# Both layer norms of a token step moved from VectorE to ScalarE, with their biases made on GpSimd

## The chip, the cores and the metric

The kernel is one program on one core of a Trainium2 chip. The time is the device time of one execution in microseconds (us). Five engines work in parallel, each through its own queue in program order: TensorE (PE, with its weight loads as PEld), VectorE (DVE), ScalarE (ACT), GpSimd (POOL) and SyncE (SP, which issues DMAs).

## The reference, cut to what matters

32 sequences of 256 steps with 64 channels pass a convolution of 9 taps (248 tokens of 128 features remain), then a Mamba-2 block and a mixture-of-experts block, both on normalised tokens and both added to the residual stream.

```python
def _layernorm(x, axis=-1, eps=1e-05):
    m = jnp.mean(x, axis=axis, keepdims=True)
    v = jnp.var(x, axis=axis, keepdims=True)
    return (x - m) / jnp.sqrt(v + eps)
...
h = _L0_tok_ref(x, ...)                         # convolution, tanh, bias, relu
h = h + _L0_attn_ref(_layernorm(h, axis=-1), ...)   # in_proj, conv, scan, gate, out_proj
h = h + _L0_ffn_ref(_layernorm(h, axis=-1), ...)    # layer_norm again, router, 2 of 16 experts, shared MLP
```

`_L0_ffn_ref` itself returns its input plus the experts' output, and begins with another layer norm of its already normalised input; the kernel makes one factor for both norms (`rs8[:, 4:8]`) and one for the single norm (`rs8[:, 0:4]`).

## The kernel before, in words

The work has three blocks behind a short setup. The first block (the profile's 28 to 655 us) is the one that changes. Its work is cut into 16 units of two sequences (496 tokens, 4 chunks of 124), and a hand-written software pipeline runs `STEPS` = 22 steps t. In step t unit a = t is convolved, unit b = t - 1 is projected, unit c = t - 2 is scanned and gated, and unit d = t - 3 is normalised for the experts; on GpSimd units t - 5 and t - 6 are scattered. Steps 0 to 2 fill the pipeline, steps 3 to 15 are full, steps 16 on drain it. The order within a step is written out by hand for each engine, and semaphores (`S.…`) tie the engines together. In steps 5, 7, 9, 11, 13, 15, 17 and 18 VectorE also picks the experts (`choose`, `slots`).

The functions that the prediction speaks of, in the order of a step:

- **ScalarE**: `silu(b, k)` empties one projection's bank after another and signals `ip_used`; `square(c, n)` waits for GpSimd's gate; `silu` of k = 2 stands behind `square(c, 0)`; `stage(d)` copies the normalised rows for the scatter.
- **TensorE**: `x_rows(b)` (L706) transposes what `silu(b, 2)` wrote, and waits for it. `output(c)` (L761, L768) ends with the sums of squares, for which it waits for VectorE's `sum_squares` (L1185). `hh_transposes` (L783) needs the rows of `normed`, `hn_transposes` (L657) those of `norm`.
- **VectorE**: `stats(a)` makes mean and variance `mv` of unit a, `norm(a)` (L1104) writes `hn`. `new_stats(c)` makes `MV` and the variances `ve8` (L1215); one step later `normed(d)` (L1224) writes `x_st`, and two small operations make `r1p` and `nmr`, scale and bias of the residual input.
- **GpSimd**: `rstd_of(a)` (L1001, L1002), `rs8_of(c)` (L1030) and `rr_of(c)` (L1026) raise to the power -1/2; `exp_of` (L997) and `decay_of` (L1010) use the same power instruction; `add_bias(a)` (L990) stands before the relu; `gate(c, n)` (L1020) multiplies with silu(z); `scatter` (L1043) issues 8 indirect DMAs for a unit, four at the end of a step and four early in the next one.

A helper `link` puts a semaphore on an instruction and lets its own engine wait for it.

Of the kernel before, what the change touches and what calls it, by code (L numbers as in the profile page):

```python
# [74 lines left out]
def audio_tower(nc, x2, tok_kernel, tok_bias, in_proj, conv_w, conv_b, dt_bias, A_log, D_skip, norm_w,  # L75
# [5 lines left out]
    ALU = mybir.AluOpType  # L81
# [39 lines left out]
    with ctx:  # L121
# [47 lines left out]
        nmr = sb("nmr", [CH, NCH])  # L169
        m1 = sb("m1", [CH, NCH])  # L170
# [19 lines left out]
        ARENA = 31560  # L190
# [197 lines left out]
        with nc.Block() as block:  # L388
# [102 lines left out]
            def _(dve):  # L491
# [37 lines left out]
                for n, (full, (hi, lo)) in enumerate(splits):  # L529
# [9 lines left out]
                 "spare_filled st_zeroed ve8_ready rs8_ready xst_ready aff_ready hhT_psum hhT_ready lg_psum "  # L539
# [28 lines left out]
        with nc.Block() as block:  # L568
# [308 lines left out]
            def _(act):  # L877
# [22 lines left out]

                def hnT_copy(a):
# [52 lines left out]
                def residual_input(d):  # L954

                    act.wait_ge(S.aff_ready, d + 1)
# [5 lines left out]
                for t in range(STEPS):  # L962
                    a, b, c, d = at(t, 0), at(t, 1), at(t, 2), at(t, 3)
                    if b is not None: silu(b, 0)
                    if a is not None: x_copy(a)
                    if b is not None: silu(b, 1)
# [6 lines left out]
                    if d is not None: shared_silu(d)  # L973
                    if c is not None: square(c, 1)
# [9 lines left out]
            def _(pool):  # L984
# [14 lines left out]
                def rstd_of(a):  # L999
                    pool.wait_ge(S.stats_ready, a + 1)  # L1000
                    link(pool, S.pool_link, nc.gpsimd.tensor_tensor(ve, mv[:, :, 1], eps_row[0:CH, 0:4], ALU.add))  # L1001
                    nc.gpsimd.tensor_tensor(rstd, ve, minus_half[0:CH, 0:4], ALU.pow)\  # L1002
                        .then_inc(S.rstd_ready, 1)
# [24 lines left out]
                def rs8_of(c):  # L1028
                    pool.wait_ge(S.ve8_ready, c + 1)
                    nc.gpsimd.tensor_tensor(rs8[:, :], ve8[:, :], minus_half[0:CH, 0:8], ALU.pow)\  # L1030
                        .then_inc(S.rs8_ready, 1)
# [39 lines left out]
            def _(dve):  # L1071
# [27 lines left out]

                def norm(a):  # L1100
                    dve.wait_ge(S.rstd_ready, a + 1)
                    later(dve, S.hnT_psum, a)
                    for j in range(4):
                        last = V.tensor_scalar(hn[:, j, :], Hb[:, 4 * F * a + j * F:4 * F * a + (j + 1) * F],  # L1104
                                               mv[:, j, 0:1], rstd[:, j:j + 1], ALU.subtract, ALU.mult)
                    last.then_inc(S.hn_ready, 1)

# [111 lines left out]
                def normed(d):  # L1219
                    dve.wait_ge(S.rs8_ready, d + 1)  # L1220
                    if d >= NXS:
                        dve.wait_ge(scattered[d % NXS], 128 * (d // NXS))
                    for j in range(4):
# [70 lines left out]
                for t in range(STEPS):  # L1294
# [11 lines left out]
                    if d is not None: normed(d)  # L1306
# [337 lines left out]
```

## Time and profile before

| | |
|---|---|
| median of 3 runs | 1109.75 us (1108.16 to 1110.27) |
| the profiled execution's own time | 1112.74 us |
| its span, first to last instruction | 1111.0 us |
| mean granted TensorE clock | 0.944 |
| busy share of the span: PE, DVE, ACT, POOL | 85%, 67%, 40%, 51% |

The span is what the trace covers; the profiled execution's own time has 1.7 us around it. The clock is given as a share of 2.4 GHz: 1.00 is 2.4 GHz, 0.50 is 1.2 GHz, and a value between them is a stretch with both. A busy share is an average over blocks with different limits.

### The profile page before, as it was taken

The page shows a single profiled execution, that of the slowest core. Times are in us where ns is not written, and L with a number is a line of the kernel's source. Part 1 is how long each engine was busy: PE and PEld are TensorE (multiplying, and loading weights), DVE is VectorE, ACT ScalarE, POOL GpSimd, SP SyncE. Part 2 cuts the span into 40 slices and gives each one's busy share as a digit, 9 for nine tenths or more (in the row PEclk, how much of TensorE's full clock was granted, in tenths as well). Part 3 has the DMA queues.
Part 4 walks back from the last instruction along what each step waited for, and adds up shares of the span by engine and source line. Part 5 has one row for each costly group of instructions (what it writes and reads, how often), then busy time and mean ns, then how long its engine had stood idle before and what let it go on. Part 6 is the DMA issues. An engine that isn't in the chain of part 4 may idle for free. (4 is left out here: it accounts for less than half of the span.)

```text
span 1111.0 us, 22688 instructions
## 1 busy us (share of the span) xinstructions
PE 948.3 (85%) x6371; PEld 795.0 (72%) x6372; DVE 746.7 (67%) x2288; ACT 441.8 (40%) x1068; POOL 572.2 (51%) x531
## 2 busy tenths in 40 slices
PE   0499999999999999999887429999999999388887
PEld 0377877877777777778665229999999999266665
DVE  4348779788797797978866615555555555488884
ACT  3233443343433333423322215555555555144443
POOL 3044444665676556775655735555555555243342
PEclk9899999999999999999986659999999999699999
DMA  6400000000000000000036422222222221223331
GB/s 134 104 20 10 1 10 11 29 20 22 17 29 29 22 24 12 29 20 17 12 95 201 137 69 61 55 63 60 63 66 62 66 62 49 74 56 91 92 92 37
DMA packets 71868, 58.97 MB, mean 53 GB/s; under 512 B 18992, under 2 KB 61291, under 8 KB 71808
## 3 DMA queue, kind: packets, MB, share of 16 engines
q1 hardware_dynamic: 63264, 41.88, 14.4%
q0 software_dynamic: 8544, 16.34, 4.4%
q8 instruction: 32, 0.52, 0.2%
q14 instruction: 28, 0.23, 0.1%
HBM read 35.62 MB, written 23.81 MB: 53 GB/s over the span
## 5 line engine op out<-in xcount | busy, mean ns | idle before, releaser
L1429 POOL DMA_INDIRECT y_tokens<-arena x139 | 155.9, 1122 | 144.7 <-DVE arena L1452 111.3
L1416 ACT ACTIVATE arena<-psum,arena 128x128 f32<-128x128 f32 x556 | 158.6, 368 | 132.0 <-PE psum L1390 130.8
L1390 PE MATMUL psum<-arena 128*128 128x128 f32 x1112 | 155.9, 284 | 3.5 <-DVE arena L1447 1.2
L1390 PEld LDWEIGHTS psum<-arena 128*128 128x128 f32 x1112 | 137.1, 194 | 16.2 <-issue 8.3
L1403 PE MATMUL psum<-arena 128*128 x1112 | 147.8, 275 | 0.4 <-ACT arena L1416 0.4
L1043 POOL DMA_INDIRECT x_slots<-arena,idx x128 | 127.3, 994 | 35.9 <-issue 35.9
L1444 DVE COPY arena<-arena 128x644 f32 x139 | 69.3, 499 | 109.5 <-DVE arena L1452 89.8
L1403 PEld LDWEIGHTS psum<-arena 128*128 128x128 f32 x1112 | 136.0, 193 | 0.6 <-issue 0.6
L623 PE MATMUL psum<-hnT_hi,w_tap_hi 128*128 128x496 f32 x192 | 80.3, 418 | 0.0
L1152 DVE TENSOR_TENSOR_SCAN arena<-psum,arena 124x496 f32<-124x496 f32 x64 | 72.4, 1173 | 6.7 <-PE psum L736 6.7
L624 PE MATMUL psum<-hnT_lo,w_tap_hi 128*128 128x496 f32 x192 | 75.8, 395 | 0.0
L625 PE MATMUL psum<-hnT_hi,w_tap_lo 128*128 128x496 f32 x192 | 75.3, 392 | 0.0
L1452 DVE TENSOR_TENSOR arena<-psum,arena 128x128 f32<-128x128 f32 x139 | 40.6, 292 | 40.2 <-PE psum L1403 38.3
L1603 ACT ACTIVATE arena<-psum,b_f 128x496 f32<-128x496 f32 x64 | 43.1, 673 | 58.0 <-PE psum L1584 58.0
L1020 POOL TENSOR_TENSOR arena<-arena 128x496 f32<-128x496 f32 x32 | 40.8, 1274 | 42.8 <-DVE arena L1178 42.8
L1494 POOL TENSOR_TENSOR rs<-ve,minus_half 124x4 f32<-124x4 f32 x16 | 16.3, 1018 | 88.9 <-DVE ve L1536 88.9
L1576 PE MATMUL psum<-w_f,arena 128*124 128x128 f32 x512 | 59.6, 275 | 1.1 <-ACT arena L1603 0.8
L1542 DVE TENSOR_SCALAR arena<-arena,mv,rs 124x128 f32<-124x128 f32 x64 | 48.3, 813 | 18.1 <-POOL rs L1494 18.1
L1576 PEld LDWEIGHTS psum<-w_f,arena 128*124 128x124 f32 x512 | 57.1, 187 | 4.6 <-issue 3.0
L1447 DVE TENSOR_SCALAR arena<-psum,lng,lnb 128x128 f32<-128x128 f32 x139 | 56.4, 406 | 5.4 <-PE psum L1397 5.4
L997 POOL TENSOR_TENSOR arena<-euler,arena 124x16 f32<-124x16 f32 x16 | 47.8, 2987 | 20.9 <-DVE arena L1118 20.8
L1584 PE MATMUL psum<-arena,w_f 128*128 128x496 f32 x128 | 57.5, 593 | 0.9 <-ACT arena L1594 0.9
(249 smaller groups left out, 2051.2 us busy)
## 6 DMA issues: line engine op xcount, KB each, us to landing
arena<-x_slots SPq DMA_DIRECT2D x139, 64.5 KB
arena<-y_tokens SPq DMA_DIRECT2D x16, 448.0 KB
arena<-in_x SPq DMA_DIRECT2D x16, 256.0 KB, 2.9
out_tokens<-arena SPq DMA_DIRECT2D x16, 224.0 KB
arena<-in_ew SPq DMA_DIRECT2D x1, 2304.0 KB
y_tokens<-arena POOLq DMA_INDIRECT x139
x_slots<-zero_src SPq DMA_DIRECT2D x33, 64.5 KB, 2.7
arena<-in_x SPq DMA_DIRECT2D x4, 512.0 KB, 6.7
```

Source lines behind the costliest of these rows:

```text
L623: nc.tensor.matmul(o, stationary[0], moving[0], start=start, stop=False)
L624: nc.tensor.matmul(o, stationary[0], moving[1], start=False, stop=False)
L625: return nc.tensor.matmul(o, stationary[1], moving[0], start=False, stop=stop)
L1043: nc.gpsimd.indirect_dma_start(out=x_slots, out_offset=bass.IndirectOffsetOnAxis(ap=idx[g % 2][:, col:col + 1], axis=0), in_=x_st[u % NXS] ...
L1152: V.tensor_tensor_scan(L0.rearrange("p h t -> p (h t)")[:, g * 2 * L:(g + 1) * 2 * L], psum[0:CH, 5 + g, 0:2 * L], diag2.rearrange("p h t ...
L1390: last = nc.tensor.matmul(psum[:, 2 + b.q % 2, k * 128:(k + 1) * 128], w1_blk[b.q % 4][:, k * 128:(k + 1) * 128], hT[b.q % 2], start=True, ...
L1403: last = nc.tensor.matmul(psum[:, 4 + c.q % 2, 0:F], EHT[c.q % 2][:, k * 128:(k + 1) * 128], w2[:, ds(at + k * F, F)], start=(k == 0), sto ...
L1416: last = nc.scalar.activation(EHT[t.q % 2][:, k * 128:(k + 1) * 128], psum[:, 2 + t.q % 2, k * 128:(k + 1) * 128], ACT.Silu, bias=w1_blk[t ...
L1429: nc.gpsimd.indirect_dma_start(out=y_tokens, out_offset=bass.IndirectOffsetOnAxis(ap=xb[t.q][:, F:F + 1].bitcast(i32), axis=0), in_=YO[t.q ...
L1444: nc.vector.tensor_copy(w1_blk[t.q % 4], w1[:, ds(at, EW)]).then_inc(X.w1_ready, 1)
L1576: last = nc.tensor.matmul(psum[0:CH, 5, j * F:(j + 1) * F], FH[:, k, j * CH:(j + 1) * CH], w_f2[:, k, :], start=(k == 0), stop=(k == NF - 1))
L1584: nc.tensor.matmul(psum[:, 1 + k, 0:UT], w_f1[:, k * 128:(k + 1) * 128], fhT, start=True, stop=True).then_inc(D.up_psum, 1)
```

## The change

`norm(a)` and `normed(d)` leave VectorE. ScalarE computes them as `Identity(scale * x + bias)` with scale rstd and bias minus mean times rstd. GpSimd makes the biases (`nmn`, `nm2`), and also `nmr` and `r1p`. A step has 8 ScalarE activations more, 10 VectorE operations fewer, and on GpSimd 2 operations and one `link` more in `rstd_of`, 4 operations and one `link` more in `rs8_of`. `rs8_ready` is now signalled by the last of them; the semaphore `aff_ready` is gone. The new waits on `hn_ready` and `xst_ready` let GpSimd overwrite the factors only after their last use.

```diff
+        nmn = sb("nmn", [CH, 4])
+        neg = sb("neg", [CH, 4])
+        neg8 = sb("neg8", [CH, 4])
+        nm2 = sb("nm2", [CH, 4])
...
-        ARENA = 31560
+        ARENA = 31544
...
+                def norm(a):
+                    act.wait_ge(S.rstd_ready, a + 1)
+                    later(act, S.hnT_psum, a)
+                    for j in range(4):
+                        last = nc.scalar.activation(hn[:, j, :], Hb[:, 4 * F * a + j * F:4 * F * a + (j + 1) * F],
+                                                    ACT.Identity, scale=rstd[:, j:j + 1], bias=nmn[:, j:j + 1])
+                    last.then_inc(S.hn_ready, 1)
+
+                def normed(d):
+                    act.wait_ge(S.rs8_ready, d + 1)
+                    if d >= NXS:
+                        act.wait_ge(scattered[d % NXS], 128 * (d // NXS))
+                    for j in range(4):
+                        last = nc.scalar.activation(x_st[d % NXS][0:CH, j, 0, 0:F],
+                                                    Hb[:, 4 * F * d + j * F:4 * F * d + (j + 1) * F],
+                                                    ACT.Identity, scale=rs8[:, 4 + j:5 + j], bias=nm2[:, j:j + 1])
+                    last.then_inc(S.xst_ready, 1)
...
                     if b is not None: silu(b, 0)
                     if a is not None: x_copy(a)
+                    if d is not None: normed(d)
                     if b is not None: silu(b, 1)
...
                     if d is not None: shared_silu(d)
+                    if a is not None: norm(a)
                     if c is not None: square(c, 1)
...
                 def rstd_of(a):
                     pool.wait_ge(S.stats_ready, a + 1)
+                    later(pool, S.hn_ready, a)
+                    nc.gpsimd.tensor_scalar(neg[:, :], mv[:, :, 0], -1.0, 0.0, ALU.mult, ALU.add)
                     link(pool, S.pool_link, nc.gpsimd.tensor_tensor(ve, mv[:, :, 1], eps_row[0:CH, 0:4], ALU.add))
-                    nc.gpsimd.tensor_tensor(rstd, ve, minus_half[0:CH, 0:4], ALU.pow)\
-                        .then_inc(S.rstd_ready, 1)
+                    link(pool, S.pool_link, nc.gpsimd.tensor_tensor(rstd, ve, minus_half[0:CH, 0:4], ALU.pow))
+                    nc.gpsimd.tensor_tensor(nmn[:, :], neg[:, :], rstd, ALU.mult).then_inc(S.rstd_ready, 1)
...
                 def rs8_of(c):
                     pool.wait_ge(S.ve8_ready, c + 1)
-                    nc.gpsimd.tensor_tensor(rs8[:, :], ve8[:, :], minus_half[0:CH, 0:8], ALU.pow)\
+                    later(pool, S.xst_ready, c)
+                    g = slice(4 * c, 4 * c + 4)
+                    nc.gpsimd.tensor_scalar(neg8[:, :], MV[:, g, 0], -1.0, 0.0, ALU.mult, ALU.add)
+                    link(pool, S.pool_link, nc.gpsimd.tensor_tensor(rs8[:, :], ve8[:, :], minus_half[0:CH, 0:8],
+                                                                    ALU.pow))
+                    nc.gpsimd.tensor_tensor(nm2[:, :], neg8[:, :], rs8[:, 4:8], ALU.mult)
+                    nc.gpsimd.tensor_tensor(nmr[:, g], neg8[:, :], rs8[:, 0:4], ALU.mult)
+                    nc.gpsimd.tensor_scalar(r1p[:, g], rs8[:, 0:4], 1.0, 1.0, ALU.mult, ALU.add)\
                         .then_inc(S.rs8_ready, 1)
...
-                def norm(a):
-                    dve.wait_ge(S.rstd_ready, a + 1)
-                    later(dve, S.hnT_psum, a)
-                    for j in range(4):
-                        last = V.tensor_scalar(hn[:, j, :], Hb[:, 4 * F * a + j * F:4 * F * a + (j + 1) * F],
-                                               mv[:, j, 0:1], rstd[:, j:j + 1], ALU.subtract, ALU.mult)
-                    last.then_inc(S.hn_ready, 1)
...
                     if c is not None: decayed_scores(c, 0)
-                    if d is not None: normed(d)
                     if m is not None: choose(m)
...
                     if c is not None: skip_add(c, 1)
-                    if a is not None: norm(a)
                     if b is not None: x_scale(b)
```

GpSimd's queue at the turn from one full step to the next, before: the power that makes `rs8`, then the first four scatters, the power of `exp_of`, four more scatters, `add_bias` and `gate(c, 0)`.

```order
L1026 TENSOR_TENSOR arena<-arena,minus_half 124x4 [waits a_ms_ready]
L1030 TENSOR_TENSOR rs<-ve,minus_half 124x8 [waits a_ve8_ready]
L1043 DMA x_slots<-arena,idx 131200x129 [waits a_idx_ready,a_staged]
L1043 DMA x_slots<-arena,idx 131200x129 x3
L997 TENSOR_TENSOR arena<-euler,arena 124x16 [waits a_nab_ready]
L1043 DMA x_slots<-arena,idx 131200x129 x4
L990 TENSOR_TENSOR arena<-arena,tokb 124x512 [waits a_h_ready,a_tanh_done]
L1020 TENSOR_TENSOR arena<-arena 128x2x248 [waits a_sq_ready,a_po_ready,a_t_ready]
```

The same place of the same queue with the change.

```order
L1052 TENSOR_TENSOR arena<-arena,minus_half 124x4 [waits a_ms_ready]
L1058 TENSOR_SCALAR neg<-MV 124x4 [waits a_xst_ready,a_ve8_ready]
L1059 TENSOR_TENSOR rs<-ve,minus_half 124x8
L1061 TENSOR_TENSOR nm<-neg,rs 124x4 [waits a_pool_link]
L1062 TENSOR_TENSOR nmr<-neg,rs 124x4
L1063 TENSOR_SCALAR r1p<-rs 124x4
L1076 DMA x_slots<-arena,idx 131200x129 [waits a_idx_ready,a_staged]
L1076 DMA x_slots<-arena,idx 131200x129 x3
L1021 TENSOR_TENSOR arena<-euler,arena 124x16 [waits a_nab_ready]
L1076 DMA x_slots<-arena,idx 131200x129 x4
L1014 TENSOR_TENSOR arena<-arena,tokb 124x512 [waits a_h_ready,a_tanh_done]
L1046 TENSOR_TENSOR arena<-arena 128x2x248 [waits a_sq_ready,a_po_ready,a_t_ready]
```

One operation now stands ahead of the power and three, behind a `link`, between it and the scatters; everything behind them in the queue has moved down by four instructions.

ScalarE's queue from the copy of x to `stage(d)`, before.

```order
L881 ACTIVATE xT_hi<-psum 128x512 [waits a_convT_psum,a_xT_psum]
L917 ACTIVATE arena<-psum,cb 128x496 [waits a_ip_ready]
L942 ACTIVATE arena<-row_ids 124x8 [waits a_xst_ready]
L944 ACTIVATE arena<-arena 124x4x128
L887 ACTIVATE arena<-psum 128x496 [waits a_conv_done,a_convT_psum]
```

The same place with the change: the four activations of `normed` (L918) stand between the copy and `silu(b, 1)`, and wait for `rs8_ready`.

```order
L885 ACTIVATE xT_hi<-psum 128x512 [waits a_convT_psum,a_xT_psum]
L918 ACTIVATE arena<-Hb,nm,rs 124x128 [waits scattered2,a_rs8_ready]
L918 ACTIVATE arena<-Hb,nm,rs 124x128 x3
L939 ACTIVATE arena<-psum,cb 128x496 [waits a_ip_ready]
L964 ACTIVATE arena<-row_ids 124x8 [waits a_xst_ready]
L966 ACTIVATE arena<-arena 124x4x128
```

The wait for `rs8_ready`, which VectorE's queue had, is now in ScalarE's, with `silu(b, 1)` behind it.

## Rows read from the trace of the kernel before

**Rows 1.** The page, part 1: busy time of each engine.
```profile
PE 948.3 (85%) x6371; PEld 795.0 (72%) x6372; DVE 746.7 (67%) x2288; ACT 441.8 (40%) x1068; POOL 572.2 (51%) x531
```
**Rows 2.** Busy time by stretch, steps 4 and 9: us, PE, PEld, DVE, ACT, POOL, clock.
```profile
135.20:166.90 31.70, 31.42 (x203) 25.63 (x203) 25.30 (x79) 12.93 (x26) 13.96 (x11) 1.00 0.03 9
304.00:337.90 33.90, 31.84 (x211) 26.03 (x211) 30.51 (x99) 12.54 (x25) 21.92 (x19) 1.00 0.08 24
```
**Rows 3.** Timeline of TensorE, the waits of full steps: start, us, what, [idle before].
```profile
188.85 1.94 PE L706 MATMUL psum<-ident,arena 128*124 128x128 f32 x8 [2.13 <-DVE arena L1158]
...
267.02 1.03 PE L768 MATMUL psum<-ones_col,arena 128*124 128x1 f32 x8 [0.29 <-DVE arena L1185]
...
291.79 1.09 PE L706 MATMUL psum<-ident,arena 128*124 128x128 f32 x8 [2.08 <-ACT arena L917]
...
325.42 1.09 PE L706 MATMUL psum<-ident,arena 128*124 128x128 f32 x8 [1.59 <-ACT arena L917]
...
359.32 1.85 PE L706 MATMUL psum<-ident,arena 128*124 128x128 f32 x8 [2.08 <-ACT arena L917]
...
394.60 1.09 PE L706 MATMUL psum<-ident,arena 128*124 128x128 f32 x8 [1.55 <-ACT arena L917]
```
**Rows 4.** Timeline of GpSimd in step 9.
```profile
306.84 1.64 POOL L1030 TENSOR_TENSOR rs<-ve,minus_half 124x8 f32<-124x8 f32 x1 [3.90 <-DVE ve L1215]
308.65 1.06 POOL L1043 DMA_INDIRECT x_slots<-arena,idx  x1 [0.17 <-issue]
...
312.56 0.97 POOL L1043 DMA_INDIRECT x_slots<-arena,idx  x1 [0.30 <-issue]
313.55 3.01 POOL L997 TENSOR_TENSOR arena<-euler,arena 124x16 f32<-124x16 f32 x1
...
322.87 1.29 POOL L1020 TENSOR_TENSOR arena<-arena 128x496 f32<-128x496 f32 x1
```
**Rows 5.** Timeline of ScalarE in step 9.
```profile
310.94 0.68 ACT L917 ACTIVATE arena<-psum,cb 128x496 f32<-128x496 f32 x1 [2.10 <-PE psum L625]
...
324.18 0.62 ACT L928 ACTIVATE arena<-arena 128x496 f32<-128x496 f32 x1 [0.57 <-POOL arena L1020]
...
334.12 1.65 ACT L959 ACTIVATE Hb<-Hb,nmr,r1p 124x128 f32<-124x128 f32 x4
```
**Rows 6.** Timeline of VectorE in step 9.
```profile
312.63 1.11 DVE L1224 TENSOR_SCALAR arena<-Hb,MV,rs 124x128 f32<-124x128 f32 x4
...
313.84 0.27 DVE L1256 TENSOR_REDUCE m<-LG 124x8 f32<-124x128 f32 x1
...
320.53 0.85 DVE L1178 SCALAR_TENSOR_TENSOR arena<-arena,d_col,psum 128x248 f32<-128x248 f32 x2
```
**Rows 7.** Timeline of GpSimd in step 1: three small operations.
```profile
71.24 0.22 POOL L1012 TENSOR_TENSOR arena<-arena,keep 124x16 f32<-124x16 f32 x1
71.42 0.20 POOL L1001 TENSOR_TENSOR arena<-arena,eps_row 124x4 f32<-124x4 f32 x1
71.70 1.01 POOL L1002 TENSOR_TENSOR arena<-arena,minus_half 124x4 f32<-124x4 f32 x1
```
**Rows 8.** Line 458, the setup's tensor_scalar on GpSimd: duration ns min/median/max.
```profile
L458 POOL TENSOR_SCALAR a_neg<-a_neg x4: 223/398/777, 22.7 to 24.2; 124x4 f32<-124x4 f32 x4
```
**Rows 9.** Busy time and granted clock in two us behind a wait of `x_rows`.
```profile
189.00:191.00 2.00, 2.00 (x9) 1.92 (x10) 2.00 (x5) 0.00 (x0) 1.04 (x2) 0.50 0.03 8
...
292.00:294.00 2.00, 2.00 (x12) 1.28 (x10) 1.26 (x10) 0.40 (x2) 1.92 (x3) 1.00 0.00 0
...
496.30:498.30 2.00, 2.00 (x9) 1.92 (x10) 1.31 (x11) 0.25 (x1) 1.92 (x2) 0.50 0.04 8
```
**Rows 10.** Timeline of TensorE, steps that fill and drain: start, us, what, [idle before].
```profile
73.92 0.64 PE L657 MATMUL psum<-ident,arena 124*128 124x124 f32 x4 [0.84 <-DVE arena L1104]
...
553.10 0.64 PE L783 MATMUL psum<-ident,arena 124*128 124x124 f32 x4 [2.79 <-DVE arena L1224]
...
586.57 1.09 PE L783 MATMUL psum<-ident,arena 124*128 124x124 f32 x4 [7.14 <-DVE arena L1224]
```

More of the change, by code:

```diff
@@ L538, in audio_tower @@
                  "po_used dve_link pool_link "
-                 "spare_filled st_zeroed ve8_ready rs8_ready xst_ready aff_ready hhT_psum hhT_ready lg_psum "
+                 "spare_filled st_zeroed ve8_ready rs8_ready xst_ready hhT_psum hhT_ready lg_psum "
                  "lg_ready up_psum up_used ffn_scaled down_psum moe_ready staged mask_ready ranks_psum "
@@ L954, in residual_input @@
                 def residual_input(d):
-                    act.wait_ge(S.aff_ready, d + 1)
+                    act.wait_ge(S.rs8_ready, d + 1)
                     for j in range(4):
@@ L1216, in new_stats @@
                         .then_inc(S.ve8_ready, 1)
[L1219 to L1223, printed above, removed]
-                        last = V.tensor_scalar(x_st[d % NXS][0:CH, j, 0, 0:F],
-                                               Hb[:, 4 * F * d + j * F:4 * F * d + (j + 1) * F],
-                                               MV[:, 4 * d + j, 0:1], rs8[:, 4 + j:5 + j],
-                                               ALU.subtract, ALU.mult)
-                    last.then_inc(S.xst_ready, 1)
-                    V.tensor_scalar(r1p[:, 4 * d:4 * d + 4], rs8[:, 0:4], 1.0, None, ALU.add)
-                    V.scalar_tensor_tensor(nmr[:, 4 * d:4 * d + 4], MV[:, 4 * d:4 * d + 4, 0], -1.0, rs8[:, 0:4],
-                                           ALU.mult, ALU.mult).then_inc(S.aff_ready, 1)
                 def logits(d):
```

## The prediction

> **What bounds the kernel now.** I read the page first. Part 1 names TensorE as busiest and VectorE after it [rows 1], but that mixes three blocks, and the change touches only the first. So I read it by step. In step 4, which has neither scatters nor `choose`, TensorE works 31.42 of 31.70 us and VectorE 25.30: TensorE is the bound. Step 9 takes 33.90 us with 31.84 us of TensorE work and 21.92 of GpSimd work, against 13.96 [rows 2]. So with the scatters about two us a step are a wait. The reader is to see that VectorE, the engine that is relieved, has slack in both.
>
> TensorE's timeline says where the wait is: ahead of the transposes of `x_rows` (L706). It lasts 2.08 us in even steps and 1.59 in odd ones, ended by ScalarE's L917, and 2.13 us in step 5, ended by VectorE's L1158 [rows 3]. There are eleven such waits in steps 5 to 15, six of 2.08 to 2.21 us and five of 1.55 to 1.61; all but that of step 5 end with L917. I follow L917 back. It stands behind `square(c, 0)`, which starts at 324.18 when GpSimd's gate ends [rows 5]; the gate starts at 322.87 and takes 1.29 us. GpSimd was idle for 3.90 us before its `rs8` power at 306.84, and from there to the gate's end at 324.16 works without a gap but for the issue times: power, four scatters, power, four scatters, `add_bias`, gate [rows 4]. This run of 17.3 us starts when VectorE's `ve8` is ready, which follows TensorE's L768. The loop is: L768, statistics, GpSimd's run, square, silu, `x_rows`, and TensorE's own work to the next L768. What is added to GpSimd's run lengthens the step one for one; what is taken from VectorE beside it does not shorten it.
>
> **The change, part by part.**
>
> *GpSimd's run, `rs8_of`.* Four small operations and a link come in, all ahead of the scatters. Of one small operation the rows show 0.18 us from start to start (71.24 to 71.42), and 0.28 where a link follows (71.42 to 71.70), 0.08 more than its 0.20 [rows 7]. So: `neg8` 0.18, link 0.08, `nm2` 0.18, `nmr` 0.18, `r1p` 0.20, together 0.82, taken as 0.8. Two of the four are tensor_scalar, whose only rows are 0.22 to 0.78 us, median 0.40 [rows 8]; they are from the cold setup, so I take the shortest, near which the warm two-input operations lie. If it is the median, the sum is 0.8 + 2 x 0.2 = 1.2; if small operations overlap, I put 0.5 as the lower end. Ten steps (6 to 15) have the whole loop: **+8.0 us** (5 to 12). The wait of `x_rows` grows to about 2.9 and 2.4 us.
>
> *The clock.* Behind three of the six waits of 2.08 us and more the granted clock is 0.50 (1.2 GHz), behind the other three 1.00 (2.4 GHz); behind the five shorter ones it is 1.00 [rows 9]. Such a fall costs 1.65 us: from `x_rows` to `x_rows` the interval is 35.28 us after 359.32, where the transposes took 1.85 us for 1.09, and 33.63 after 291.79 [rows 3]. All ten waits would now be longer than 2.08 us. With the frequency of the six it falls in 5 of the 10, at most in all; I take 7. Step 5 loses its own fall with its wait (below). Against three falls now that is four more: **+6.6 us** (+3 to +12).
>
> *VectorE loses `normed`, `r1p` and `nmr`:* from 312.63 to 313.84, 1.2 us in each step, ahead of `skip_add(c, 0)` and the second scans [rows 6]. It counts only where VectorE's queue ends the wait, in step 5: **-1.2 us**. In step 9 `skip_add` ends at 321.38 and the gate starts at 322.87 [rows 4, 6], so nothing is gained.
>
> *VectorE loses `norm`* between `skip_add(c, 1)` and `x_scale`. Then `sum_squares`, which stands behind `x_scale`, comes earlier, and the wait of 0.29 us before L768 in the five odd steps goes [rows 3]: **-1.5 us** (0 if `square(c, 1)` becomes as late).
>
> *ScalarE gains two groups of four activations.* The same form, two pointer operands over 124 x 128, is L959: four take 1.65 us [rows 5], against 1.11 for VectorE's four [rows 6]. `normed` waits for `rs8_ready`, at 306.84 + 0.18 + 1.64 + 0.08 + 0.56 = 309.3, and ends at 311.0. It fills ScalarE's idle 2.10 us; `silu(b, 1)` started at 310.94 [rows 5], so it is 0.1 us late, and its reader on TensorE, `projection(b, 2)`, stands behind the convolution. If that cover went, 0.1 us a step would be paid. `norm(a)` lies between `shared_silu` and the wait for `gate(c, 1)`. Queued behind it are `square(c, 1)`, `silu(b, 4)` and the copy of hnT; the hn_transposes are last in TensorE's step. Full steps: 0.
>
> *Filling.* In steps 0 and 1 TensorE waits for `norm` itself (0.84 us in step 1) [rows 10]. There GpSimd adds 0.18 + 0.08 + 0.20 and ScalarE 1.65 - 1.11 = 0.54: +1.0 in step 0. In step 1 `silu(b, 4)`, two activations of about 0.68 us [rows 5], now stands behind `norm` and ahead of the hnT copy. Norm's end moves from 73.86 to 74.86, the silus end at 76.2; before, the transposes ended at 73.92 + 0.64 = 74.56. That is +1.7. **+2.7 us** (1.5 to 4).
>
> *Draining.* In steps 16 and 17 no convolution covers `normed`, and TensorE waits for VectorE's L1224, 2.79 and 7.14 us [rows 10]. On ScalarE `normed` doesn't stand behind VectorE's scans and products, so these end about 2 us sooner; the products behind them are held by VectorE's own queue, 1.2 us shorter. I take -1.2 for step 16 and -2.1 for step 17, and +0.8 for the four operations of the last `rs8_of`, with the last scatters behind them: **-2.5 us** (-4 to +1, since clock and GpSimd's run act here too).
>
> The other two blocks are untouched: 0. **Sum:** 8.0 + 6.6 - 1.2 - 1.5 + 2.7 - 2.5 = +12.1 us. On the profiled execution's own 1112.74 us (span 1111.0, 1.7 around it) that gives 1124.8; it lies 3.0 above the median, so for the median I forecast 1109.75 + 12.1 = 1121.9 us.
>
> **The rivals.**
>
> 1. *The loop lengthens, the clock doesn't fall more often:* 12.1 - 6.6 = +5.5, 1115.3 us. For it: three of six waits were harmless. Against: the rise takes every wait past those that were followed by a fall.
> 2. *Everything at its upper end:* 12 for the operations, 11.6 for the clock, +3 for the rest: 1136 us. For it: rows 8.
> 3. *The small operations are nearly hidden,* 0.3 us a step: +3 with no more falls, -1.2 - 1.5 + 2.7 - 2.5: +0.5, 1110.3 us, no change. Against: [rows 7].
> 4. *Faster, by relieved contention.* VectorE's `normed` runs beside GpSimd's run. If it held GpSimd up, its going would give back up to its 1.11 us a step; from 0.8 us on that outweighs the four operations. At 1.11: -0.3 x 10 and the rest of the direct terms, -2.5: 1104 us. Against: the scatter at 312.56, which runs beside L1224 at 312.63, takes 0.97 us, and the one at 308.65, with no such neighbour, 1.06 [rows 4, 6]. The Trainium skill, GPSIMD Engine Reference, section Key points, says that GpSimd shares its SBUF interfaces with VectorE, with contention where a VectorE instruction runs in a two-port mode. By that rule this rival has a case; the trace shows no effect on the scatters.
> 5. *ScalarE gets onto the path:* both norms paid at the difference of 0.54 us in 16 units, 2 x 16 x 0.54 = +17 on the rest: 1139 us. It decides when `normed` ends later than TensorE's next need of `silu(b, 1)`. Against: 2.10 us idle [rows 5]. The Trainium skill, ScalarE: Activation LUTs, section Rules for kernel authors, wants multiplications and additions on VectorE and not on ScalarE. By that rule the move itself costs; the trace agrees for the group's duration, not for the path.
>
> **How the numbers follow.** Forecast with its spread (+7 to +20) 0.62, rival 1 0.13, rival 2 0.09, rival 3 0.08, rival 4 0.05, rival 5 0.03. Median runs differ by 0.2%, 2.2 us, without a change, which I take as the bound of "same". Slower: forecast, rivals 2 and 5 and nearly all of 1, 0.86. Same: rival 3 and a rest of 1, 0.09. Faster 0.05. The range from 1112 to 1130 holds the forecast and rival 1 and leaves out rivals 2 to 5 but for some of their edges, 0.2 in all.
>
> **What would show each step right or wrong.** GpSimd: four operations around the `rs8` power, 0.8 us longer from its start to the first scatter. TensorE: waits before `x_rows` of about 2.9 and 2.4 us, still ended by the silu behind `square(c, 0)`; none before L768. Clock: 0.50 behind about seven of these ten waits, and 1.00 in step 5, whose wait is about 0.9 us. VectorE: idle up by some 3 us a step, of use to nobody. ScalarE: `normed` from about 2.5 us after the power's start, `silu(b, 1)` late by 0.1 us. I am wrong if the wait of `x_rows` does not grow (rivals 3, 4), if it is ended by something else (5), or if the clock follows another rule than the length of the wait (1).

## The result, and the profile after

The changed kernel takes 1127.95 us, the median of 4 runs (1126.39 to 1129.36), against 1110.01 for the kernel before beside it (1108.16 to 1113.96, 4 runs): ratio 1.0162, 95% interval 1.0138 to 1.0185, slower by 17.9 us. The forecast was 1121.9 with a range of 1112 to 1130. The kernel before takes 1107.4 to 1110.3 us in some executions (mean granted clock 0.947 to 0.954) and 1112.7 to 1114.6 in the others (0.941 to 0.945), and its profiled one, 1112.74, is of the longer ones. The two profiled executions differ by 16.6 us of span, 1127.6 against 1111.0; I account for these.

Page of the kernel after, the span and part 1, which answer to [rows 1]:

```profile
span 1127.6 us, 22782 instructions
PE 955.6 (85%) x6371; PEld 800.3 (71%) x6372; DVE 700.3 (62%) x2128; ACT 492.5 (44%) x1196; POOL 590.4 (52%) x627
```

VectorE is relieved by 46 us, ScalarE gains 51 and GpSimd 18. The kernel is slower all the same; which engine's added work makes it so, the shares don't tell.

Busy time by stretch of the kernel after, steps 4 and 9, columns as in [rows 2]:

```profile
142.20:173.50 31.30, 30.98 (x202) 25.43 (x202) 22.32 (x69) 16.09 (x33) 14.82 (x17) 1.00 0.03 9
313.00:347.00 34.00, 31.37 (x210) 25.82 (x209) 27.51 (x89) 15.77 (x33) 22.99 (x25) 1.00 0.08 24
```

Step 4 has lost nothing. In step 9 VectorE works 3 us less than before and TensorE stands longer. Where, TensorE's timeline says (start, us, what, [idle before]; answers to [rows 3]):

```profile
194.29 1.06 PE L710 MATMUL psum<-ident,arena 128*124 128x128 f32 x8 [0.88 <-DVE arena L1182]
...
299.45 1.97 PE L710 MATMUL psum<-ident,arena 128*124 128x128 f32 x8 [2.98 <-ACT arena L939]
...
335.18 1.09 PE L710 MATMUL psum<-ident,arena 128*124 128x128 f32 x8 [2.44 <-ACT arena L939]
```

`x_rows` is L710 now. Its waits grew from 2.08 to 2.98 and from 1.59 to 2.44, still ended by the silu (L939, before L917); only step 5, where VectorE ended the wait, has gained, from 2.13 to 0.88. No wait is left ahead of the sums of squares. The cause stands in GpSimd's timeline of step 10 (answers to [rows 4]):

```profile
350.01 0.19 POOL L1058 TENSOR_SCALAR neg<-MV 124x4 f32<-124x4 f32 x1 [3.91 <-DVE ve L1239]
350.16 1.64 POOL L1059 TENSOR_TENSOR rs<-ve,minus_half 124x8 f32<-124x8 f32 x1
351.88 0.20 POOL L1061 TENSOR_TENSOR nm<-neg,rs 124x4 f32<-124x4 f32 x1
352.03 0.20 POOL L1062 TENSOR_TENSOR nmr<-neg,rs 124x4 f32<-124x4 f32 x1
352.19 0.20 POOL L1063 TENSOR_SCALAR r1p<-rs 124x4 f32<-124x4 f32 x1
352.74 1.07 POOL L1076 DMA_INDIRECT x_slots<-arena,idx  x1 [0.35 <-issue]
```

From the run's start to its first scatter are 2.73 us, before 1.81. The small operations follow each other at 0.15 to 0.16 us, a little less than forecast, but the first scatter behind them has 0.35 us of issue for 0.17: together +0.92 for the +0.8 forecast.

ScalarE did what was expected (timeline of steps 8 and 9, answers to [rows 5]):

```profile
318.18 1.65 ACT L918 ACTIVATE arena<-Hb,nm,rs 124x128 f32<-124x128 f32 x4 [0.43 <-POOL r1p L1063]
319.85 0.68 ACT L939 ACTIVATE arena<-psum,cb 128x496 f32<-128x496 f32 x1
```

The group takes the 1.65 us of the row it was priced by, and nobody waits for the silu behind it. Two places of the timeline I had not priced right. The first is the filling (TensorE, steps 0 and 1, answers to [rows 10]):

```profile
51.28 1.09 PE L661 MATMUL psum<-ident,arena 124*128 124x124 f32 x4 [8.63 <-ACT arena L909]
...
76.28 0.64 PE L661 MATMUL psum<-ident,arena 124*128 124x124 f32 x4 [1.79 <-ACT arena L909]
...
77.53 1.18 PE L723 MATMUL psum<-arena 64*124 64x248 f32 x2 [0.60 <-ACT arena L943]
```

Behind these waits the clock falls. Busy time by stretch, the same ten us and the ten behind them, then two us behind a wait of 2.98 and one of 2.44 (answers to [rows 9]; the column behind POOL is the granted clock):

```profile
73.00:83.00 10.00, 7.61 (x35) 6.41 (x33) 2.70 (x4) 3.46 (x7) 1.39 (x4) 0.71 0.00 1
78.00:88.00 10.00, 10.00 (x39) 8.75 (x39) 6.20 (x12) 1.26 (x3) 2.90 (x1) 0.53 0.09 26
299.60:301.60 2.00, 2.00 (x9) 1.95 (x10) 1.36 (x11) 0.27 (x1) 1.92 (x2) 0.50 0.04 8
335.20:337.20 2.00, 2.00 (x11) 1.48 (x12) 1.96 (x13) 0.40 (x1) 1.92 (x2) 1.00 0.00 0
```

From 78 to 88 us TensorE is busy all the time and gets 39 matmuls done at 0.53 of the clock. The kernel before has 1.00 from 73 to 83.

The second is in a block that the change doesn't touch, the routed blocks. Busy time in 250 us of them, first of the kernel before, where TensorE works 99.3% of the time:

```profile
690.00:940.00 250.00, 248.19 (x2073) 236.85 (x2072) 135.54 (x366) 138.82 (x488) 137.40 (x123) 1.00 0.22 62
```

and 260 us of the kernel after, 98.7%:

```profile
690.00:950.00 260.00, 256.51 (x2142) 245.74 (x2141) 139.67 (x378) 144.07 (x504) 144.28 (x126) 1.00 0.22 62
```

VectorE's timeline there shows one copy in eight blocks that starts late, behind no other engine (kernel after):

```profile
762.19 0.50 DVE L1452 COPY arena<-arena 128x644 f32 x1 [1.07 <-issue]
778.73 0.50 DVE L1452 COPY arena<-arena 128x644 f32 x1 [1.08 <-issue]
```

In the kernel before, the copy at that place (L1444 at 763.50 us) has 0.99 us of idle time put down to VectorE's own work, so the copy is only some 0.1 us later here; the turn of eight blocks takes 16.41 us before and 16.53 here.

**The account.** The milestones are the starts of the hnT copy that ends each step, and the first routed block (657.64 us before, 672.95 after).

| stretch | before | after | difference | forecast |
|---|---|---|---|---|
| to step 2's copy | 102.11 | 109.31 | +7.2 | +2.7 |
| steps 3 and 4 | 64.76 | 64.23 | -0.5 | 0 |
| step 5 | 35.80 | 33.12 | -2.7 | -1.2 and a fall of the clock less |
| ten full steps | 341.18 | 353.82 | +12.6 | +8.0 -1.5 and five falls more |
| draining | 113.79 | 112.47 | -1.3 | -2.5 |
| the rest | 453.4 | 454.7 | +1.3 | 0 |

Of the +7.2, 0.7 us lie ahead of step 0's norm: TensorE starts the transposes before it (L647, now L651) at 41.30 and 41.99 us. Over all the kernels of this document that start lies between 41.30 and 43.17 us without an order by their code, so milestones of two traces compare only to 1 or 2 us unless this start is taken off. Steps 0 and 1 then have +1.0 and +1.2, and step 2, which holds the stretch at half clock, +4.3.

### The profile page after: what moved, and what is told of

Read it like the earlier page. It is cut to its first block and busy times, and to the rows that moved or that the text cites. A ratio compares the mean times of both kernels' runs of the same rounds, so it can differ in the third digit from the quotient of the medians.

```text
span 1127.6 us, 22782 instructions
## 1 busy us (share of the span) xinstructions
PE 955.6 (85%) x6371; PEld 800.3 (71%) x6372; DVE 700.3 (62%) x2128; ACT 492.5 (44%) x1196; POOL 590.4 (52%) x627
## 5 line engine op out<-in xcount | busy, mean ns | idle before, releaser
L1437 POOL DMA_INDIRECT y_tokens<-arena x139 | 158.4, 1140 | 142.7 <-DVE arena L1460 119.4
L1398 PEld LDWEIGHTS psum<-arena 128*128 128x128 f32 x1112 | 136.7, 194 | 16.6 <-issue 12.7
```

The costliest lines, as they stand in the source:

```text
L1398: last = nc.tensor.matmul(psum[:, 2 + b.q % 2, k * 128:(k + 1) * 128], w1_blk[b.q % 4][:, k * 128:(k + 1) * 128], hT[b.q % 2], start=True, ...
L1437: nc.gpsimd.indirect_dma_start(out=y_tokens, out_offset=bass.IndirectOffsetOnAxis(ap=xb[t.q][:, F:F + 1].bitcast(i32), axis=0), in_=YO[t.q ...
```

## The experiments

Each ratio is against the kernel before on the same chip; its median there was 1111.44 us for the first four experiments (16 runs of it), 1109.18 for the next four (17) and 1112.69 for the last four (23). The ratios go by the means of the runs, which move less than these medians, so a ratio can differ a little from that of the two medians. Counts of falls and waits are those of the one profiled execution of each kernel.

**e1_pad.** The kernel before with the four operations around the power, written to scratch that nobody reads:

```diff
                 def rs8_of(c):
...
+                    nc.gpsimd.tensor_scalar(neg8[:, :], MV[:, g, 0], -1.0, 0.0, ALU.mult, ALU.add)
+                    link(pool, S.pool_link, nc.gpsimd.tensor_tensor(rs8[:, :], ve8[:, :], minus_half[0:CH, 0:8],
+                                                                    ALU.pow))
+                    nc.gpsimd.tensor_tensor(nm2[:, :], neg8[:, :], rs8[:, 4:8], ALU.mult)
+                    nc.gpsimd.tensor_tensor(nmn[:, :], neg8[:, :], rs8[:, 0:4], ALU.mult)
+                    nc.gpsimd.tensor_scalar(neg[:, :], rs8[:, 0:4], 1.0, 1.0, ALU.mult, ALU.add)\
+                        .then_inc(S.rs8_ready, 1)
```

> The kernel before, in which only rs8_of gets the changed kernel's four small operations and link (their results go to scratch tiles; both norms stay on VectorE). Theory (GpSimd's run is in the loop, one for one, and the clock falls behind longer waits): the run from the rs8 power to the gate grows by 0.9 us, the ten waits of x_rows from 2.08 and 1.59 to about 2.98 and 2.45 us, +8.7 us; the clock falls behind about 7 of them for 2 before, +8; +0.9 in the last rs8_of: +17 us, 1127. Rival 3 of the prediction (small operations hidden): 0 to +2. Rival 1 (the waits grow, the falls stay): +9.6. Rival 5 (the loss of the changed kernel comes from ScalarE's queue): 0, since ScalarE has nothing new here.

Measured: 1123.44 us, ratio 1.0116 (1.0089 to 1.0143). TensorE's timeline of this kernel:

```profile
295.03 1.09 PE L710 MATMUL psum<-ident,arena 128*124 128x128 f32 x8 [3.08 <-ACT arena L921]
...
329.61 1.09 PE L710 MATMUL psum<-ident,arena 128*124 128x128 f32 x8 [2.52 <-ACT arena L921]
```

The waits are 1.0 and 0.93 us longer than before, with nothing moved between engines. So the operations alone make about seven tenths of the loss (0.0116 of 0.0162); the ten full steps take 353.8 us together, exactly what they take in the kernel after. The time lies between the theory's +17 us and the +9.6 of a loop without more falls: the clock falls in 4 of the ten full steps (one fall twice as long as the others), against 2 before and 7 after, and not in step 5. These are fewer than expected, with waits that are longer still.

**e2_norm_only and e3_normed_only.** The change in two halves. e2 takes over `norm` and `rstd_of` of the change and leaves `normed`, `r1p`, `nmr` and `rs8_of` as they were; e3 is the other half.

```diff
-                    if a is not None: norm(a)
...
+                    if a is not None: norm(a)
```

for e2 (out of VectorE's queue, into ScalarE's), and for e3

```diff
-                    if d is not None: normed(d)
...
+                    if d is not None: normed(d)
```

> The changed kernel with only norm(a) on ScalarE; normed(d), nmr and r1p are VectorE's and rs8_of is the one of before. Theory: the ten waits are as before (2.08 and 1.59 us) with two falls of the clock; the waits ahead of L768 go, -4 us over ten steps; filling costs +7 as in the changed kernel (norm waits in steps 0 and 1 and a low clock of 10 us behind them): +3 us, 1113. If filling's low clock is an accident of the changed kernel and not norm's doing: -1 us, 1109. If ScalarE's norm holds the loop: +8 or more.

> The changed kernel with only normed(d) on ScalarE and its four operations in rs8_of; norm(a) is VectorE's. Theory: +8.7 for GpSimd's run, +8 for five more falls of the clock, -2.9 in step 5, -1.3 in draining, nothing in filling and nothing at L768: +12.5 us, 1122.5. Rival (the two norms' costs are not separable, as when VectorE's relief by norm matters for the loop): e2 and e3 don't add up to the changed kernel's +17.9 us within 3.

Measured: e2 1116.26 us, 1.0050 (1.0033 to 1.0068); e3 1123.77 us, 1.0118 (1.0092 to 1.0144). The sum, 4.8 + 12.3 = 17.1 us, is within 1 us of the whole change's 17.9. e3 has the filling of before and waits of 2.97 to 3.03 and 2.43 to 2.47 (3.28 in step 6). It came out at the +12.5 expected, but with 4 falls in the ten full steps and not 7; three of them last twice as long, so the match is in part luck. e2 has the filling of after, with its stretch at half clock, and the waits of before. Its steps without a fall take 33.4 us, before 33.61 and 33.95: the move of `norm` alone gives back 0.2 us in even and 0.55 in odd steps. Yet its ten full steps together are only 0.6 us shorter, since the clock fell in 4 of them where 2 were expected; so e2 lost 4.8 us and not the 3 of its theory.

**e4_fill.** The kernel after, with `norm` of units 0 and 1 back on VectorE, GpSimd's operations left in:

```diff
-                    if a is not None: norm(a)
+                    if a is not None and a > 1: norm(a)
...
                     if c is not None: skip_add(c, 1)
+                    if a is not None and a < 2: norm(a)
```

> The changed kernel, but norm of units 0 and 1 is computed on VectorE as before (GpSimd's operations stay). Theory: TensorE's waits in steps 0 and 1 shrink by about 0.6 and 1.5 us and the low clock of 10 us in step 2 goes with them: -6 us against the changed kernel, 1122. Rival (the fall in step 2 has another cause, or comes at random): -1 to -2 us only, with 0.50 still in the clock of step 2.

Measured: 1125.18 us, 1.0131 (1.0104 to 1.0158). The waits in the filling went only to 8.09 and 1.25 us, the clock still fell at 77 us (6.8 us for 10.2), and step 2's copy came at 106.33 for 109.31. I had expected 6 us and no fall; the fall stayed, as the rival had it, and about half of the 6 us came. The rest was to be looked for in `rstd_of`, and e9 does.

**e5_bias_vector.** The kernel after, but the three products stand on VectorE in place of `normed`, and `rs8_of` is the one power again:

```diff
+                def biases(d):
+                    dve.wait_ge(S.rs8_ready, d + 1)
...
+                    V.scalar_tensor_tensor(nm2[:, :], MV[:, 4 * d:4 * d + 4, 0], -1.0, rs8[:, 4:8],
+                                           ALU.mult, ALU.mult)
+                    V.tensor_scalar(r1p[:, 4 * d:4 * d + 4], rs8[:, 0:4], 1.0, None, ALU.add)
+                    V.scalar_tensor_tensor(nmr[:, 4 * d:4 * d + 4], MV[:, 4 * d:4 * d + 4, 0], -1.0, rs8[:, 0:4],
+                                           ALU.mult, ALU.mult).then_inc(S.aff_ready, 1)
```

> The changed kernel (both norms on ScalarE), but the second norm's three small results nm2, r1p and nmr are made on VectorE where normed stood, and rs8_of is one power again. Theory: GpSimd's run is as before, the ten waits of x_rows are 2.08 and 1.57 us again; the relief ahead of L768 (-4) and filling (+7, as far as it comes from norm on ScalarE) stay; step 5 gains about 0.9 of VectorE's 1.2: like e2_norm_only or 1 us less, +3 to +5 us against before. Rival (normed on ScalarE itself costs, not its operations on GpSimd): as the changed kernel, +17.

Measured: 1114.53 us, 1.0037 (1.0013 to 1.0061), as the theory had it. TensorE's timeline:

```profile
330.20 1.09 PE L710 MATMUL psum<-ident,arena 128*124 128x128 f32 x8 [1.44 <-ACT arena L939]
...
363.53 1.09 PE L710 MATMUL psum<-ident,arena 128*124 128x128 f32 x8 [1.89 <-ACT arena L939]
```

The waits are 1.88 to 2.10 and 1.44, step 5 has 0.87, the full steps take 33.3 to 33.5 us but for one with a fall of the clock, and the ten together are 5.6 us shorter than before. Both norms on ScalarE cost nothing in a full step; making the second norm's biases on GpSimd does. What is lost lies in the filling (step 2's copy at 109.00, +6.9) and in draining (+1.6).

**e6_scatter_before, e7_scatter_after, e8_scatter_normed.** Half the scatters of the run moved behind GpSimd's `exp_of` to both sides of the gate, in the kernel before, the kernel after and e3:

```diff
-                    if v is not None and v < UNITS - 5: scatter(v, (2, 3))
...
+                    if v is not None and v < UNITS - 5: scatter(v, (2,))
...
+                    if v is not None and v < UNITS - 5: scatter(v, (3,))
```

> The kernel before, with the four scatters that stood between exp_of and add_bias moved behind the gate: two ahead of gate(c, 1), two behind it. Theory: GpSimd's run is 5 us shorter and no longer ends the wait of x_rows; in even steps the wait of 2.08 us goes, in odd steps VectorE's scans end it, at 1 to 2.1 us as in step 5; fewer falls of the clock: -10 to -17 us, 1095 to 1101. Rival (the scatters only move the delay to gate(c, 1) and to L761, TensorE's output): within 3 us of before, with new waits at L761 or L768.

> The changed kernel with the same move of the scatters. Theory: its four operations in rs8_of are off the loop, and VectorE's relief of 1.2 us now shortens the waits of the odd steps to 0.9 us as in its step 5; filling's +7 stays: within 4 us of e6_scatter_before, so that the change costs next to nothing there, against +17.9 in its own place. Rival (the change costs its 0.9 us a step wherever the scatters stand): e6 plus 15 or more.

> e3_normed_only (normed on ScalarE, norm on VectorE) with the same move of the scatters. Theory: VectorE's relief in the odd steps without filling's cost: 4 to 8 us faster than e6_scatter_before, and the fastest of all, 1088 to 1095. Rival (VectorE's relief has no value here either): same as e6.

Measured: 1120.02 us, 1.0084 (1.0055 to 1.0112); 1130.65 us, 1.0183 (1.0157 to 1.0209); 1124.97 us, 1.0134 (1.0107 to 1.0162). All three theories missed, e6's by 19 us and e8's by 30; all three kernels are slower than the kernel before, and e7 is 10.6 us above e6, between its theory (4) and its rival (15). My picture of a single chain was too simple. Timeline of TensorE in e6:

```profile
328.59 1.06 PE L706 MATMUL psum<-ident,arena 128*124 128x128 f32 x8 [2.14 <-DVE arena L1159]
336.65 2.01 PE L761 MATMUL psum<-arena 128*124 128x128 f32 x16 [0.96 <-POOL arena L1020]
338.97 1.03 PE L768 MATMUL psum<-ones_col,arena 128*124 128x1 f32 x8 [0.31 <-DVE arena L1186]
```

The same wait is now ended by VectorE's scans. Beside the chain over gate, square and silu runs a second one from the same GpSimd run over `exp_of`, VectorE's `dt_rest` and the scans, hardly shorter. It has the four operations ahead of `exp_of` too. An even step of e6, then the same step of e7:

```profile
293.41 1.06 PE L706 MATMUL psum<-ident,arena 128*124 128x128 f32 x8 [1.61 <-DVE arena L1159]
...
300.67 1.94 PE L710 MATMUL psum<-ident,arena 128*124 128x128 f32 x8 [2.44 <-DVE arena L1183]
```

In even steps the wait grows by 0.83 us with the four operations. In odd steps, where VectorE also has `choose`, it shrinks from 2.14 to 1.92: there VectorE's relief presumably outweighs them. And the gate of the next half, pushed back, got a wait of its own on TensorE, 0.96 us.

**e9_fill_full.** e4, and `rstd_of` of units 0 and 1 in its old form as well:

```diff
+                    if a < 2:
+                        nc.gpsimd.tensor_tensor(rstd, ve, minus_half[0:CH, 0:4], ALU.pow)\
+                            .then_inc(S.rstd_ready, 1)
+                    else:
```

> The changed kernel, but for units 0 and 1 the norm stands on VectorE and GpSimd's rstd_of is the short one of the kernel before (no negated mean, no product); from unit 2 on everything is as changed. Theory (the filling cost 7.2 us: about 3 us of longer waits of TensorE for the first two hn, and about 4 us because step 1 then runs a stretch at half clock): the waits of hn_transposes in steps 0 and 1 go back near 7.4 and 0.6 us, no fall of the clock before step 2, step 2's hnT_copy starts near 102 to 103 us, and the time is 6 to 7 us below the changed kernel's 1128, 1121 to 1122. Rival (the half-clock stretch at 77 us isn't from these waits, since the kernel in which only the norm was moved back still had it): 3 to 4 us below, about 1124, with the fall still there.

Measured: 1119.91 us, 1.0083 (1.0055 to 1.0110). The waits are back at 7.66 and 0.81, step 2's copy at 103.00, and no fall of the clock; in the same ten us as above the trace of e9 has:

```profile
73.00:83.00 10.00, 9.19 (x56) 7.58 (x55) 8.12 (x16) 3.09 (x6) 2.38 (x2) 1.00 0.09 27
```

The theory holds: the stretch at half clock comes with waits of 8.63 and 1.79 us (after, e2, e5, e7) and of 8.09 and 1.25 (e4), and with 7.7 and 0.8 us it is absent from all nine kernels that have them. It cost more than the waits did. Against the kernel after the span is 8.8 us shorter. 6.3 of it are the filling; 5.0 more come from the ten full steps, which the edit does not touch, with 4 falls for 7, and 2.4 are lost again behind them.

**e10_best.** e5 with e9's filling: everything that the runs had shown to cost is undone, what paid is kept.

> Both norms on ScalarE, the three bias operations (nm2, r1p, nmr) on VectorE behind the reciprocal roots, rs8_of the single power of the kernel before, and for units 0 and 1 the norm on VectorE with the short rstd_of. Theory (what makes the change slow are GpSimd's four small operations in front of the scatters and the two first norms; the rest is worth about 2.7 us in step 5 and 0.2 to 0.3 us a step): the filling as before, waits of x_rows 1.9 to 2.1 and 1.4 us, 0.9 us in step 5, time 1103 to 1106, faster than before by 0.4 to 0.6%. Rival (the falls of the clock come and go with the phase of the loop, so that a shorter loop can have as many as the kernel before or more): 1108 to 1113, no difference.

Measured: 1116.09 us, 1.0034 (1.0012 to 1.0055). The theory missed by 10 us. The rival's 1108 to 1113 was nearer, but still 3 us short, and it names only half of the reason. The span is 3.8 us longer than that of the kernel before: 2.1 shorter to step 15's copy (541.80 against 543.85), 0.9 longer in draining, and 5.0 longer behind it. The falls of the clock took some 5 us of the gain in the ten full steps, five for two. The other 5.0 were lost where nothing had been changed, in the routed blocks (e10):

```profile
690.00:940.00 250.00, 242.89 (x2030) 231.79 (x2030) 133.19 (x359) 136.76 (x479) 134.54 (x120) 1.00 0.22 61
```

2030 matmuls for the 2073 of the kernel before; the part from the first routed block to the end takes 458.4 us for 453.4.

**e11_pad8.** e1 with each of the four operations twice, to see the dose:

```diff
+                    nc.gpsimd.tensor_scalar(neg8[:, 4:8], MV[:, g, 0], -1.0, 0.0, ALU.mult, ALU.add)
...
+                    nc.gpsimd.tensor_tensor(nm2[:, 4:8], neg8[:, 4:8], rs8[:, 4:8], ALU.mult)
+                    nc.gpsimd.tensor_tensor(nmn[:, 4:8], neg8[:, 4:8], rs8[:, 0:4], ALU.mult)
+                    nc.gpsimd.tensor_scalar(neg[:, 4:8], rs8[:, 0:4], 1.0, 1.0, ALU.mult, ALU.add)
```

> The kernel before with eight small GpSimd operations to scratch around the power in rs8_of (four of them gave ratio 1.0116); nothing else is moved and nobody reads them. Theory (each of the small operations lengthens every one of the steps 3 to 12 by its own duration and what lies around it, 0.2 to 0.25 us, and the clock adds what its falls cost): waits of x_rows 3.8 to 4.1 and 3.4 us, steps without a fall 1.8 to 2.0 us longer than before, +18 to +20 us from the loop alone and 1128 to 1138 in all with the falls of the clock. Rival (behind the first 0.8 us another track bounds the loop, or the small operations overlap): waits below 3.6 us and less than 1128.

Measured: 1130.80 us, 1.0182 (1.0154 to 1.0209). The time is what the theory gave, the waits are not: GpSimd's timeline of this kernel shows why.

```profile
314.11 0.19 POOL L1035 TENSOR_SCALAR neg<-MV 124x4 f32<-124x4 f32 x1 [3.92 <-DVE ve L1229]
314.26 0.19 POOL L1036 TENSOR_SCALAR neg<-MV 124x4 f32<-124x4 f32 x1
...
317.25 1.07 POOL L1057 DMA_INDIRECT x_slots<-arena,idx  x1 [0.16 <-issue]
```

Run's start to first scatter is 3.14 us: +1.33 for eight operations, +0.92 for four. The waits are 3.4 to 3.6 and 2.8 us. An operation costs 0.15 us, and the extra 0.2 us of issue ahead of the scatter, which after and e1 have, is gone here. So e1's microsecond is four times 0.15, the link, and 0.2 of issue that four operations brought and eight did not. The clock made up the rest of the time, with six falls in steps 5 to 15 for three.

**e12_norm_from2.** The kernel before with `norm` on ScalarE from unit 2 on: the one part of the change that pays, alone.

> The kernel before with only the norm of units 2 and later on ScalarE (negated mean and its product on GpSimd there); units 0 and 1 and normed are as in the kernel before. Theory (moving the norm alone cost 4.8 us, because the filling lost about 6 to 7 us with its fall of the clock while the full steps gained 0.2 us each): the filling as before, time 1107 to 1110, 0 to 3 us below the kernel before. Rival (the more frequent falls of the clock in steps 3 to 12 that the run with the norm alone had, five against three, were its cost): 1112 to 1115 with four to five falls in the steps.

Measured: 1114.82 us, 1.0032 (1.0016 to 1.0049). The clock fell in four of the ten full steps, so the rival has both its time (within 1112 to 1115) and its falls. But it does not have the place of the loss: as in e10 the milestones are ahead of the profiled kernel before to the end of the first block, falls included, step 15's copy at 540.44 (-3.4) and the first routed block at 654.40 (-3.2), and the rest takes 458.2 us (+4.8). This compares one execution of each kernel; how many falls the others had is not known. TensorE's timeline there has what the kernel before doesn't show in these 45 us at all:

```profile
762.00 1.13 PE L1409 MATMUL psum<-arena 128*128 128x128 f32 x8 [0.41 <-DVE arena L1463]
778.78 1.13 PE L1409 MATMUL psum<-arena 128*128 128x128 f32 x8 [0.36 <-DVE arena L1463]
795.57 1.13 PE L1409 MATMUL psum<-arena 128*128 128x128 f32 x8 [0.36 <-DVE arena L1463]
```

and VectorE's the copy that they wait for:

```profile
777.87 0.50 DVE L1463 COPY arena<-arena 128x644 f32 x1 [1.23 <-issue]
```

Neither expectation, of e10 or e12, had allowed for this. A turn of eight blocks takes 16.78 us for 16.41, and the block loop makes some 17 turns. Over all the kernels the turn goes with VectorE's program ahead of the loop. It takes 16.41 us in the kernel before, e1, e6 and e11, whose VectorE code is the same; 16.53 to 16.55 in the kernel after and e7, which share theirs; 16.51 in e3 and e8, which do too; 16.6 in e4 and e9 likewise; 16.56 in e2, 16.75 in e10, 16.79 in e12, and 16.41 again in e5. GpSimd's program differs within these groups and the turn hardly does. That the place of the loop in VectorE's instruction stream does it is an inference from this pattern; no run changed the place alone.

## Why the prediction was right, and where its terms were off

The measured 1127.95 us lies in the range, 6 us above the forecast's 1121.9.

**The mechanism and the bound** were right: TensorE's wait ahead of `x_rows`, GpSimd's run behind it, and VectorE's slack, whose 46 us of relief bought a few. e1 shows GpSimd's part without the move of the norms, e5 the move without GpSimd's part.

**GpSimd's run, +8.0.** Measured +0.92 from its start to the first scatter and +0.87 to the gate, so +8.7. The forecast's 0.82 was near for a wrong reason: operations of 0.15 rather than 0.18, and 0.2 of issue that it had not foreseen. The upper bound of 1.2, from the setup's tensor_scalar rows, was not needed: in the full steps these take 0.19.

**The clock, +6.6.** Seven of ten waits with a fall, as forecast, and none in step 5; a step with a fall takes about 1.6 us longer (e12: 35.05 for 33.39), so five more in the full steps and one less in step 5 are the 6.6. But the rule behind it, that longer waits bring more falls, did not hold: e1 and e3 with waits of about 3.0 and 2.5 us had 4 of ten each, some of them twice as long; e10 fell behind each of its five waits of 1.85 to 2.06 us, e5 behind one of its five of the same length. The size was right by luck. Where the falls come from beyond the wait is open; e10's come every second step, 68.3 us apart, so some relation of the loop's time to a period of the clock's control is likely, but not shown. The Trainium skill, TensorE: Matmul & The Clock Gate, section What's actually happening, says that the chip decides on a time grid of its own that doesn't start with the kernel. The trace agrees as far as the same wait is followed by either level.

**VectorE loses `normed`, -1.2,** in step 5 only: the wait there went from 2.13 to 0.88, -1.25. Right; with the fall that went, step 5 is 2.7 us shorter.

**VectorE loses `norm`, -1.5.** Mis-sized: -3.9. e2, e5 and e12 have full steps of 33.3 to 33.5 us, falls left aside, for 33.61 and 33.95. I had counted the 0.29 us ahead of L768 in odd steps; the even steps gained 0.2 too, and the odd 0.55. What the rest of the gain goes through, no run isolates.

**ScalarE, 0 in full steps.** Right; rival 5 fell with e5.

**Filling, +2.7.** This is the term that failed by most: +7.2, or +6.5 without the 0.7 that lie ahead of step 0's norm. The waits grew as I had worked out, by about 1 us in each step; steps 0 and 1 are 2.2 us longer together. What the term had left out is that the clock can fall in the filling as well: 10.2 us at half clock, in a step 2 that takes 4.3 us more. e9 undid both.

**Draining, -2.5.** -1.3. The waits of `hh_transposes` (now L787) that I had priced, in steps 16 and 17, went from 2.79 to 0.54 and from 7.14 to 5.07, -2.2 and -2.1 for the forecast's -1.2 and -2.1. But the third, in step 18, grew from 5.35 to 6.50, and between the first two `x_rows` got a wait of 5.23 us where the kernel before has none; neither was in my sum. The kernel before, then the kernel after:

```profile
617.26 1.09 PE L783 MATMUL psum<-ident,arena 124*128 124x124 f32 x4 [5.35 <-DVE arena L1224]
...
581.53 1.96 PE L710 MATMUL psum<-ident,arena 128*124 128x128 f32 x8 [5.23 <-ACT arena L939]
...
601.96 1.09 PE L787 MATMUL psum<-ident,arena 124*128 124x124 f32 x4 [5.07 <-ACT arena L918]
...
633.52 1.09 PE L787 MATMUL psum<-ident,arena 124*128 124x124 f32 x4 [6.50 <-ACT arena L918]
```

**The other two blocks, 0.** +1.3 here, and 5 us in e10 and e12. That these blocks are untouched holds for their code; that they therefore cost 0 was wrong.

In e1 the clock fell 4 times for 3 in steps 5 to 15, near what rival 1 supposed; the changed kernel had 7. Rival 2's upper ends were not reached: the operations cost 0.9 us and not 1.2, and three of the ten waits had no fall. Rival 3 fell with e1. Rival 4 asked for the contention of VectorE and GpSimd: where I looked GpSimd was not held, but VectorE was, below. Terms off by 0.5 to 4.5 us with both signs left the sum 4.5 us short of the profiled 16.6. That they partly cancel, and that the clock's term came out, is luck; the loop's +8.7 is not.

## What to carry to other kernels

Before moving work to an idle engine, price what the move adds to the engine on the path, here 0.9 us of operations on four columns in a run that ten steps go through: the relief of an engine with slack bought less. Put such helper operations where the slack is (e5), and take the units of the filling out of a rule that was made for the full steps (e9). A kernel that comes out neither faster nor slower may have gained in its own stretch and lost in another, so lay the milestones of two traces side by side before giving up a version.

## What the runs showed of the hardware that I had not expected

A VectorE instruction can be held for a whole GpSimd instruction. In e6 GpSimd's `add_bias`, two inputs of 124x512, ran first (its timeline and VectorE's):

```profile
321.09 1.27 POOL L990 TENSOR_TENSOR arena<-arena,tokb 124x512 f32<-124x512 f32 x1 [1.92 <-ACT arena L893]
```

```profile
321.14 1.25 DVE L1128 TENSOR_SCALAR arena<-arena 124x16 f32<-124x16 f32 x1
```

The same tensor_scalar of 16 columns takes 0.17 us in step 9 of the kernel before (L1127 at 318.54), and GpSimd's 1.27 is the median of its sixteen. In the kernel before `norm` met the gate in the same way in each step from 2 on (VectorE's timeline in step 9, then GpSimd's):

```profile
330.75 2.05 DVE L1104 TENSOR_SCALAR arena<-Hb,arena 124x128 f32<-124x128 f32 x4
```

```profile
330.91 1.29 POOL L1020 TENSOR_TENSOR arena<-arena 128x496 f32<-128x496 f32 x1 [1.76 <-DVE arena L1178]
```

One of the four takes 1.28 us and the others 0.33 to 0.34; in steps 0 and 1, which have no gate, the four take 1.11. So `norm` weighed 2.05 us on VectorE in a full step, and not the 1.11 of its own work. Whether this is why taking it off gave more than forecast was not tested. The Trainium skill, SBUF — State Buffer, section Who interferes with whom, has the rule: where both want the shared ports, these are locked for an instruction, and whichever engine issues second is blocked. The trace agrees in both places; the forecast had cited the contention from another page and looked only for GpSimd being held.

The half clock comes in pieces of very different length behind similar waits: 3.4 us behind most waits of 1.9 to 3 us in full steps, 6.8 us behind some (step 10 of e1, three steps of e3), and 10.2 us behind the 1.79 and 0.60 us at the end of step 1 of the kernel after. What sets the length is not shown.
